# Edge gathers of 126 rows in place of 128 in a graph network kernel

## The reference

```python
m = xl[src] + xr[dst]                       # xl = x @ Wl, xr = x @ Wr
e = leaky_relu(m, 0.2)
logits = einsum('ehc,hc->eh', e, att)
alpha = softmax of logits over the edges with one dst
out = segment_sum(alpha * xl[src], dst) + bias_conv
y = elu(graph_norm(out));  x1 = layernorm(x + y)
```

```python
for l in range(2):                          # h = x1 at first
    msg = sum_b comp[l][etype][:, b] * (h[src] @ basis[l, b])
    h = tanh(segment_sum(msg, dst) + h @ loop_w[l] + bias[l])
out = layernorm(x1 + h)
```

## Time and profile before

| | |
|---|---|
| median of three runs | 3581.94 us |
| the profiled execution | 3583.63 us, its span 3581.8 us |
| TensorE | 2957.1 us busy, 83% |
| VectorE | 2565.8 us, 72% |
| GpSimd | 2222.8 us, 62% |
| ScalarE | 1815.4 us, 51% |
| bytes moved by DMA | 579.28 MB, mean 162 GB/s |
| granted TensorE clock, mean | 0.935 of full speed |

### The profile page before, as it was taken

One profiled execution on the slowest core, in us unless ns is written; L12 is line 12 of the kernel. 1 busy time (PEld: TensorE's weight loads), 2 busy tenths in 40 slices (PEclk: granted clock), 3 DMA queues, 4 the chain that ended last, 5 costly groups with the idle time before them and its releaser, 6 DMA issues. The chain is left out here.

```text
span 3581.8 us, 65764 instructions
## 1 busy us (share of the span) xinstructions
PE 2957.1 (83%) x17251; PEld 2212.4 (62%) x17251; DVE 2565.8 (72%) x8027; ACT 1815.4 (51%) x4346; POOL 2222.8 (62%) x2605
## 2 busy tenths in 40 slices
PE   4787888878775788788869999969979999967776
PEld 4777777777774555477745555548855555545654
DVE  4777777777775798877757777734447777758887
ACT  2444444444442344389956666634436666635554
POOL 6777777777773122278877777712247777726666
PEclk9899898999887899999989999989989999989998
DMA  4455555444442788678823333359943333349886
GB/s 100 121 127 124 123 123 129 124 121 128 122 123 71 210 247 245 193 258 271 270 92 104 103 103 104 105 166 301 299 150 104 103 103 104 104 143 291 280 281 202
DMA packets 647622, 579.28 MB, mean 162 GB/s; under 512 B 74323, under 2 KB 534484, under 8 KB 647252
## 3 DMA queue, kind: packets, MB, share of 16 engines
q1 hardware_dynamic: 494436, 335.02, 31.6%
q0 software_dynamic: 82688, 207.65, 20.9%
q10 hardware_dynamic: 70128, 32.39, 3.3%
HBM read 366.34 MB, written 208.43 MB: 160 GB/s over the span
## 5 line engine op out<-in xcount | busy, mean ns | idle before, releaser
L1867 DVE SCALAR_TENSOR_TENSOR work<-bank,coef,work 128x128 f32<-128x128 f32 x2400 | 673.9, 342 | 244.7 <-ACT work L1308 241.0
L1032 PE MATMUL bank<-basis_s,work 128*128 128x512 f32 x1600 | 755.9, 595 | 1.5 <-ACT work L1301 1.5
L744 POOL DMA_INDIRECT work<-in_x_dram,slot_src x400 | 423.4, 1059 | 130.9 <-issue 121.6
L744 POOL DMA_INDIRECT work<-in_x_dram,slot_dst x400 | 417.8, 1045 | 122.0 <-issue 122.0
L793 POOL DMA_INDIRECT work<-h_d,slot_src x400 | 384.4, 961 | 132.0 <-issue 121.7
L793 POOL DMA_INDIRECT work<-x_d,slot_src x400 | 383.9, 960 | 132.0 <-issue 121.7
L1308 ACT ACTIVATE work<-bank,coef 128x128 f32<-128x128 f32 x800 | 294.1, 368 | 224.7 <-PE bank L1032 224.7
L1032 PEld LDWEIGHTS bank<-basis_s,work 128*128 128x128 f32 x1600 | 274.3, 191 | 196.6 <-issue 192.6
L758 POOL DMA_DIRECT2D conv_d<-work x99 | 74.0, 751 | 325.3 <-DVE work L1756 315.9
L1078 PE MATMUL bank<-work,loop_s 128*128 128x512 f32 x392 | 213.8, 627 | 73.5 <-ACT work L1349 73.4
L1043 PEld LDWEIGHTS bank<-work 128*126 128x126 f32 x1600 | 206.9, 189 | 101.6 <-issue 100.9
(11 more groups left out here) (273 smaller groups left out, 7835.4 us busy)
## 6 DMA issues: line engine op xcount, KB each, us to landing
w_d<-work SPq DMA_DIRECT2D x800, 62.5 KB
work<-in_x_dram SPq DMA_DIRECT2D x194, 256.0 KB, 3.1
work<-x_d SPq DMA_DIRECT2D x194, 256.0 KB, 4.0
w_d<-work SPq DMA_DIRECT2D x400, 66.9 KB
work<-w_d SPq DMA_DIRECT2D x398, 64.0 KB, 3.2
work<-w_d ACTq DMA_DIRECT2D x390, 64.0 KB, 3.3
xl_d<-work SPq DMA_DIRECT2D x97, 256.0 KB
work<-xl_d SPq DMA_DIRECT2D x97, 256.0 KB, 3.8
```

The costliest lines, as they stand in the source:

```text
L744: pool.indirect_dma_start(quad(k, i % 3)[:, c, :], None, x, bass.IndirectOffsetOnAxis(ap=table[:, a:a + 1], axis=0)).then_inc(e_in[i % 3], 16)
L1032: pe.matmul(psum[YBANKS[k % 5]][:, :], quad(1, i % 2)[:, c, :], basis_s[:, l, :, :].rearrange("k b n -> k (b n)"), start=True, stop=True). ...
L1867: ins = dve.scalar_tensor_tensor(o, psum[YBANKS[k % 5]][:, b * D:(b + 1) * D], coef[:, i, l, c, b:b + 1], o, ALU.mult, ALU.add)
```

## The change

The two places that issue gathers in the edge stretches name partitions 0 to 125 of the destination and of the index table instead of all 128. Partitions 126 and 127 of `work[0]` and `work[1]` then keep what stood there, and TensorE still transposes 128 partitions; so that this is a number from the start, VectorE clears partitions 96 to 127 of both buffers once, ahead of its wait for the tables. The four gathers by `tile_at` (line 749) are as before.

```diff
@@ attention stretch, GpSimd
-                        pool.indirect_dma_start(quad(k, i % 3)[:, c, :], None, x,
-                                                bass.IndirectOffsetOnAxis(ap=table[:, a:a + 1], axis=0)).then_inc(e_in[i % 3], 16)
+                        pool.indirect_dma_start(quad(k, i % 3)[0:SLOTS, c, :], None, x,
+                                                bass.IndirectOffsetOnAxis(ap=table[0:SLOTS, a:a + 1], axis=0)).then_inc(e_in[i % 3], 16)
@@ layers, GpSimd
-                        pool.indirect_dma_start(quad(0, i % 3)[:, c, :], None, (x1_d, h1_d)[l],
-                                                bass.IndirectOffsetOnAxis(ap=slot_src[:, a:a + 1], axis=0)).then_inc(r["h_in"][i % 3], 16)
+                        pool.indirect_dma_start(quad(0, i % 3)[0:SLOTS, c, :], None, (x1_d, h1_d)[l],
+                                                bass.IndirectOffsetOnAxis(ap=slot_src[0:SLOTS, a:a + 1], axis=0)).then_inc(r["h_in"][i % 3], 16)
@@ start, VectorE
             st.did(dve.memset(unsorted[:, :], 0.0))
+            for k in range(2):
+                st.did(dve.memset(work[k][96:P, 0:3 * 4 * D], 0.0))
 
             dve.wait_ge(tables_in, 16 * 7)
```

## The result

The changed kernel takes 3635.52 us (median of four runs, 3629.94 to 3643.61), the kernel before 3583.93 us in the same comparison. The ratio is 1.0152, with a 95% interval of 1.012 to 1.0184: slower by 52 us, where 3577 us and a range up to 3680 us were forecast. The mean granted clock of TensorE is 0.935 in both profiles. The profiled execution of the changed kernel is 3643.6 us long, its span 3641.8 us, so 60.0 us over the span of before; it is the longest of the four.

What follows compares the result with a forecast made beforehand. GpSimd's gathers were taken to bound the attention stretch, nearly level with TensorE in the layers. 1600 gathers at -3 ns gave 4.8 us less, clears and bytes nothing: 3581.9 to 3577 us, range up to 3680 us.

Steps and rivals of the forecast that it cites:

- The bound: Edge stretches: GpSimd full of gathers at 1.356 us each in the attention stretch, nearly level with TensorE in the layers.
- The room of 10 us a layer: Layers' edge stretches: faster gathers give back at most 0.10 us a row, about 10 us a layer, before TensorE bounds.
- The clears: VectorE's start: two memsets, 2.7 us for both, inside 5.04 us of idle time, cost 0.
- the bytes: Edge-stretch gathers: 1.64 MB fewer out of 579, no DMA bound there, so no gain.
- the landing: Gathered rows' arrival, 2.8 us in the layers: an eighth later, 0.35 us, would cost under 1 us in all.
- The descriptor work: GpSimd's work on each of 1600 gathers: taken as -3 ns each, 4.8 us less in all.
- Both signs of being wrong: Gathers: median moving over 7 ns either way, or attention stretch and layers moving by unlike amounts per gather when slower.
- The rival of uneven division: Gathers' descriptor work on GpSimd: 14 engines take nine rows each, 22 to 51 ns dearer, 3617 to 3663 us; chance 0.27.
- little or no change: Whole kernel: time moves by -10 to +5 us, own range 3570 to 3588 us; chance 0.40.
- Packets: Software queue: unchanged at 82688 if sixteen engines keep at most eight rows, 19200 more if fourteen take nine.
- Faster by rows: Gathers in the edge stretches: duration goes by rows, 6.3 to 14.8 ns saved each, 3558 to 3572 us; chance 0.24.
- Piecewise, 212 ns: Gathers: a different path for counts not a multiple of 16, up to 212 ns each, 339 us, 3920 us; chance 0.09.

Runs made afterwards that it cites:

- e6: The changed kernel with 126 rows in the attention stretch's 800 gathers only, the layers' back at 128: 3613.42 us, ratio 1.0087 to the kernel before.
- e7: The changed kernel with every edge-stretch gather fetching 120 rows instead of 126, run a second time: 3629.0 us against 3579.12 for the kernel before, ratio 1.0131.
- e1: The changed kernel with its gathers back at 128 rows, so only the two clears remain: ratio 0.9979 to the kernel before.

## Why the prediction was wrong

- **The bound.** Right. GpSimd is full of gathers in all three stretches and a gather's price goes straight to the time; the starts of the gathers give 33.2 + 11.4 + 10.1 us, and e6 splits the time the same way. That the layers pay a slower gather in full was right too. The room of 10 us a layer for faster ones was never used up: in the first layer 112 rows took 4.5 us of it and 96 rows 504.7 - (2302.0 - 1804.2) = 6.9 us.
- **The clears, the bytes, the landing.** Right, at 1.34 us each in a cover of 5 us, at nothing, and at 2.8 us as before.
- **The descriptor work, taken as -3 ns: the step that failed.** I took the number of rows for what counts and stayed near zero because a store of 80 partitions was no cheaper than one of 128. But 80 is 16 x 5, and both stores leave no engine out; at best the row told what fewer rows do on sixteen engines, and nothing of fifteen. Not even that carried over: the store was 22 to 26 ns dearer, while gathers of 112 and 96 rows are cheaper than those of 128, and why the store was dearer stays open. The term measured +51 ns in the attention stretch and +39 in the layers, by medians; by means +41 and +27, which come to 54 us. By e7 38 and 33 of the medians' rise come with the sixteenth engine lost, and 13 and 6 with the ninth row. Both signs of being wrong that the prediction named came: a median moved by more than 7 ns, and unlike amounts in the stretches, the second of which isn't explained.
- **The rival of uneven division** named the mechanism, its engines (14 with nine rows) and its range: 22 to 51 ns, 3617 to 3663 us; it got 0.27. Its upper end, 51 ns for a ninth step, hit the measured median by luck. A step costs 13 ns, which the gathers of 112, 96 and 125 rows show (20 ns between 112 and 128 rows in the layers), and the greater part is a price of its own that the rival did not have. The Trainium skill (DMA: Bandwidth & Descriptors, section "Why a DMA increments its semaphore by 16 and not by 1") says that the largest number of engines up to 16 that divides the slowest dimension is the one used. The packets of four gather sizes agree for indirect copies too: 15, 14, 13 and 5 engines for 120, 126, 117 and 125 rows. The trace of before could not decide between this and sixteen engines with a share rounded up, since 128 and 80 rows come out the same either way; little or no change at 0.40 was put too high.
- **Packets.** 19200 more were foreseen for 14 engines and 25600 came; the 6400 between are those of the two engines without rows.
- **Faster by rows.** Partly real, at 13 ns for sixteen rows, 0.8 ns a row, where 3.2 to 7.4 were allowed. 126 rows on sixteen engines would have eight steps still, so by this fit even they would have gained nothing; no run shows such a gather.
- **Piecewise, 212 ns.** Not for 126 rows. With one row fewer a gather is dearer than that, 1209 - 947 = 262 ns, but by the shares of 25 rows and not by another path.

No version that computes the whole result beat the kernel before. The edge tile needs 126 rows, and of 126 and 128, the two run that hold it, 128 is the cheaper. The runs of 112 and 96 rows are faster only because they leave out edges.

## What to carry to other kernels

When GpSimd's gathers set the pace, look at the divisors of their row count: here a multiple of 16 was cheapest, and padding 126 rows up to 128 cost less than leaving two out (947 for 998 ns). Multiply what one gather changes by before believing that two rows in 128 are small. And a row from the trace bounds a new form only if it differs from the old one in the same way; 80 rows are a multiple of 16, 126 are not.

## What the runs showed of the hardware

- A gather's descriptor time on GpSimd goes by the rows of one engine's share, some 13 ns each (921, 934 and 947 ns for 6, 7 and 8 rows, 1209 for 25 on 5 engines). Where fewer than 16 engines carry rows it has 26 to 41 ns on top. The engines left out get as many packets as the others, with four bytes for each row.
- In some surroundings the kernel before takes 4019 or 3964 us. The waits of e1 (engine, line, releaser, us in total, times, longest) show the edge stretches no longer bound by GpSimd alone:

```profile
ACT work L1323 <- remote: 258.2, 58, 6.1
...
POOL work L793 <- remote: 144.4, 75, 4.1
...
POOL work L744 <- PE bank L855: 136.7, 51, 10.0
```

  Before, GpSimd waited for nothing there. With these stalls dearer gathers did no harm: 120 rows ran at 0.9838 of the time of before. The clock granted to TensorE is lower there as well, 0.908 in e1 for 0.935, which may be cause or effect. At line 1323 the program waits only for TensorE and for stores of `w_d`; before, the profile names these stores as the releaser there (20.8 us), so later stores are one candidate for the first line. Why 120 rows take less, and what "remote" stands for, stays open.
